# Where a transform's stores, its statistics and a copy of the solved block stand in a spectral convolution kernel

## The reference

```python
m = mean(g, axis=(2, 3, 4)); s = var(g, axis=(2, 3, 4))      # g: 32 groups of channels
v = (g - m) / sqrt(s + eps)
xfft = rfft2(pad(v, 1), norm='ortho')                        # 34 x 18 frequencies
vfft = rfft2(weight, s=(34, 34), norm='ortho')               # 128 x 127 at each frequency
wfft = vH @ vfft
wfft = wfft + mean(diagonal(wfft)) * 1e-5 * I
ortho = I - 2.0 * (vfft @ solve(wfft, vH))                   # cut to 128 x 128
z = irfft2(ortho @ xfft, norm='ortho')[:, :, 1:-1, 1:-1] + bias
return x + z
```

## Time and profile before

| | us |
|---|---|
| median of 3 runs | 3135.11 |
| lowest, highest | 3126.38, 3148.89 |
| the profiled execution | 3139.82 |
| its span, first to last instruction | 3137.1 |
| PE busy | 2606.8 (83%) |
| VectorE busy | 2014.0 (64%) |
| ScalarE busy | 1269.0 (40%) |
| GpSimd busy | 742.2 (24%) |

### The profile page before, as it was taken

One profiled execution on the slowest core, in us unless ns is written; L12 is line 12 of the kernel. 1 busy time (PEld: TensorE's weight loads), 2 busy tenths in 40 slices (PEclk: granted clock), 3 DMA queues, 4 the chain that ended last, 5 costly groups with the idle time before them and its releaser, 6 DMA issues. The chain is left out here.

```text
span 3137.1 us, 89161 instructions
## 1 busy us (share of the span) xinstructions
PE 2606.8 (83%) x38281; PEld 2133.8 (68%) x38281; DVE 2014.0 (64%) x3842; ACT 1269.0 (40%) x2963; POOL 742.2 (24%) x1307
## 2 busy tenths in 40 slices
PE   3994919889999888998886968778888879959999
PEld 3663915555666677877775747566676768859999
DVE  5453710779788787787778889697887782003333
ACT  0441402443534255555533534343454444632221
POOL 0340000312121042332431414031343242520000
PEclk7897969989999899999988989797988899976787
DMA  4348073314231064754733516060231232566662
GB/s 171 104 110 149 2 121 67 123 56 163 68 113 40 15 129 81 139 110 80 158 67 62 109 29 135 3 136 13 93 95 53 65 120 77 164 140 162 169 168 92
DMA packets 562599, 310.00 MB, mean 99 GB/s; under 512 B 484616, under 2 KB 495496, under 8 KB 561368
## 3 DMA queue, kind: packets, MB, share of 16 engines
q1 hardware_dynamic: 520896, 183.58, 28.5%
q0 software_dynamic: 41312, 120.73, 11.4%
HBM read 162.85 MB, written 141.30 MB: 97 GB/s over the span
## 5 line engine op out<-in xcount | busy, mean ns | idle before, releaser
L1386 DVE SCALAR_TENSOR_TENSOR arena<-arena,psum 128x512 f32<-128x512 f32 (+2 forms) x608 | 399.0, 719 | 280.2 <-PE psum L1016 279.9
L1349 DVE TENSOR_TENSOR arena<-arena 128x960 f32<-128x960 f32 (+24 forms) x480 | 420.2, 876 | 16.6
L1344 DVE TENSOR_TENSOR arena<-arena 128x960 f32<-128x960 f32 (+8 forms) x600 | 403.9, 723 | 8.3
L953 PE MATMUL psum<-arena 128*32 128x256 f32 (+1 forms) x2904 | 263.9, 430 | 90.9 <-DMA arena<-plain 73.9
L995 PEld LDWEIGHTS psum<-arena 32*32 32x32 f32 x9280 | 160.5, 118 | 256.9 <-issue 240.4
L871 POOL COPY arena<-arena 128x512 f32<-128x512 f32 (+2 forms) x160 | 87.1, 594 | 1040.0 <-ACT arena L1159 1040.0
L1016 PE MATMUL psum<-arena 32*128 32x64 f32 x9280 | 313.1, 282 | 9.8 <-ACT arena L1180 9.8
L1016 PEld LDWEIGHTS psum<-arena 32*128 32x128 f32 x9280 | 291.7, 197 | 34.5 <-ACT arena L1180 20.4
L995 PE MATMUL psum<-arena 32*32 32x64 f32 x9280 | 187.0, 235 | 135.9 <-DVEq L1378 125.7
L957 PE MATMUL psum<-arena 128*32 128x256 f32 (+1 forms) x3696 | 264.5, 373 | 0.0
L1159 ACT COPY arena<-arena 32x128 f32<-32x128 f32 (+3 forms) x496 | 222.2, 448 | 31.4 <-DVE arena L1386 12.5
(11 more groups left out here) (121 smaller groups left out, 4764.9 us busy)
## 6 DMA issues: line engine op xcount, KB each, us to landing
blocks<-arena POOLq DMA_DIRECT2D x145, 256.0 KB, 2.5
arena<-blocks SPq DMA_DIRECT2D x290, 128.0 KB, 2.8
kept<-arena POOLq DMA_DIRECT2D x145, 256.0 KB, 3.0
arena<-kept SPq DMA_DIRECT2D x145, 256.0 KB, 2.8
xhat<-arena SPq DMA_DIRECT2D x32, 580.0 KB, 13.0
arena<-xhat SPq DMA_DIRECT2D x580, 32.0 KB, 2.6
yhat<-arena POOLq DMA_DIRECT2D x290, 64.0 KB, 2.3
arena<-x SPq DMA_DIRECT2D x8, 2048.0 KB, 11.7
```

Of the source, the lines that this page charges most:

```text
L953: pe.matmul(columns[quadrant(p)].rearrange("p (a k) n -> p a k n", k=m), K["ident"][:, quadrant(p)], spread(base[:, 0:m, :], 1, n), start= ...
L1344: ins = dve.tensor_tensor(pr, spread(R[:, t, :, :, j], 3, 2 * w_), both, ALU.mult)
L1349: link(dve.tensor_tensor(rest, rest, pr[:, :, h], op))
L1386: ins = dve.scalar_tensor_tensor(old, old, K["mask"][:, piv:piv + 1], upd_bank(u, c)[:, 0:L * n].rearrange("p (t n) -> p t n", n=L), ALU.m ...
```

## The change

In block 1 VectorE makes the statistics first and the shift matrices after them. `eps_all` moves from block 1 to block 2, behind `norm(1)` of the first half. SP does not wait at the end of block 2 any more, and does not store the second half there; it stores it in the solver, behind the second load of tables, and the loads for `pre`, ScalarE's `copy_blocks` and VectorE's first `place` wait for all stores. `HOME` turns around, so that group a lies at the high end of `M`, and `ce` moves to the low end, so that forming does not touch `xs`. `copy_p` and `copy_q` move from GpSimd to ScalarE.

```diff
-HOME = [0, 82]
+HOME = [NQ - 82, 0]
...
+        def store_half(sp, h):
+            for p in range(NP):
+                for r in range(2):
+                    lo = 2 * B * (p % LB) + B * r
+                    sp.dma_start(xhat[p // LB, h, lo:lo + B, :], xs[p * B:p * B + B, r, :, :].rearrange(
+                        "i f b -> i (f b)")).then_inc(s_stored, 16)
...
                     ident_d = spread(K["ident"], 1, ND)
+                    statistics(dve, 0, link, 0)
                     dve.wait_ge(s_const, 32)
                     dve.wait_ge(s_a_copied, nbank)
...
                     dve.tensor_tensor(shift_sb, shift_sb, diag, ALU.add).then_inc(s_shift, 1)
-                    statistics(dve, 0, link, 0)
-                    dve.wait_ge(s_tab, 16)
-                    link(dve.tensor_tensor(eps_prod, eps_tab, spread(e_d, 1, NQ), ALU.mult))
-                    dve.tensor_reduce(eps_all, eps_prod, AX.X, ALU.add)
...
-                    for h in range(2):
-
-                        sp.wait_ge(s_s2_cp, 3 * (h + 1) * HALF)
-                        for p in range(NP):
-                            for r in range(2):
-                                lo = 2 * B * (p % LB) + B * r
-                                sp.dma_start(xhat[p // LB, h, lo:lo + B, :], xs[p * B:p * B + B, r, :, :].rearrange(
-                                    "i f b -> i (f b)")).then_inc(s_stored, 16)
-                    sp.wait_ge(s_stored, 16 * NP * 2 * 2)
+                    sp.wait_ge(s_s2_cp, 3 * HALF)
+                    store_half(sp, 0)
...
+                            if c == 0:
+                                dve.wait_ge(s_eps, 16)
+                                link(dve.tensor_tensor(eps_prod, eps_tab, spread(e_d, 1, NQ), ALU.mult))
+                                link(dve.tensor_reduce(eps_all, eps_prod, AX.X, ALU.add))
...
         a = Carve(BASE_SOLVE)
+        NCE = NT
+        ce = a(NCE, SP_, 2 * B)
+        M_AT = a.at
         M = a(RESIDENT, QUAD, L)
...
                         if kind in ("form", "pre"):
+                            if kind == "pre" and k == 0:
+                                sp.wait_ge(s_stored, 16 * NP * 2 * 2)
                             for n, (of, _, first, _, _, _) in enumerate(loads):
                                 if of == kind and lo <= first < hi:
                                     load_tables(n)
+                                if n == 1 and at == 0:
+                                    store_half(sp, 1)
...
                         elif kind == "mid":
-                            pool.wait_ge(S["upd_copied"], 2 * before("sweep", at))
...
                             for m in range(lo, hi):
-                                copy_p(m)
-                                if m > lo:
-                                    store_part(m - 1)
-                            store_part(hi - 1)
+                                store_part(m)
                         elif kind == "final":
-                            pool.wait_ge(S["s_done"], before("mid", at))
-                            pool.wait_ge(S["upd_copied"], 2 * before("sweep", at))
-                            for m in range(lo, min(lo + 4, hi)):
-                                copy_q(m)
                             for m in range(lo, hi):
                                 store_y(m)
-                                if m + 4 < hi:
-                                    copy_q(m + 4)
...
+                    def copy_p(m):
+                        if m >= 2:
+                            act.wait_ge(S["s_done"], m - 1)
+                        src = M[:, home(mid_quads[m]), :, :]
+                        dst = emb[:, m % 2, 1].rearrange("p f q r m -> p (f q) r m")[:, :, 0, :]
+                        act.copy(dst, src.rearrange("p f n -> p (f n)").rearrange("p (a b) -> p a b", b=B))
+                        act.copy(work[:, m % 2, :, 0:L], src).then_inc(S["p_copied"], 1)
+
+                    def copy_q(m):
+                        src = M[:, home(final_quads[m]), :, :].rearrange("p f n -> p (f n)").rearrange("p (a b) -> p a b", b=B)
+                        dst = q_emb[:, m % 4].rearrange("p f q r m -> p (f q) r m")[:, :, 0, :]
+                        act.copy(dst, src).then_inc(S["q_copied"], 1)
...
                         elif kind == "pre":
+                            act.wait_ge(s_stored, 16 * NP * 2 * 2)
...
                             copy_b(lo)
+                            copy_p(lo)
                             copy_j(lo)
                             for m in range(lo, hi):
                                 copy_t(m)
                                 if m + 1 < hi:
                                     copy_j(m + 1)
+                                    copy_p(m + 1)
                                 copy_s(m)
...
                                 for m in pairs[n + 1] if n + 1 < len(pairs) else ():
                                     copy_jq(m)
+                                    copy_q(m)
...
-                        if sj >= NCE:
+                        if sj < NCE:
+                            dve.wait_ge(s_stored, 16 * NP * 2 * 2)
+                        else:
                             dve.wait_ge(S["u_done"], set_jobs[sj - NCE][3])
```

More of the change, by code:

```diff
@@ L261, in build @@
         s_x = [ctx.enter_context(nc.semaphore(f"s_x{i}")) for i in range(4)]
-        s_mv = ctx.enter_context(nc.semaphore("s_mv"))
+        s_mv, s_eps, s_stored = (ctx.enter_context(nc.semaphore(n)) for n in ("s_mv", "s_eps", "s_stored"))
+        def store_half(sp, h):
[4 more added lines that the diff above has]
+                        "i f b -> i (f b)")).then_inc(s_stored, 16)
         def load_x(sp, h, q):
@@ L680, in build @@
         assert early.at <= a.at
-        early = Carve(BASE_SOLVE + HOME[1] * QUAD * L)
+        early = Carve(M_AT + HOME[1] * QUAD * L)
         tiles += [table(early) for _ in range(4)]
@@ L1279, in _ @@
                             act.wait_ge(S["formed"], before("form", at))
-                            act.wait_ge(S["upd_done"], before("sweep", at))
+                            act.wait_ge(S["upd_copied"], 2 * before("sweep", at))
                             copy_b(lo)
+                            copy_p(lo)
                             copy_j(lo)
```

28 lines of the change are left out of this document (7 added, 21 removed).

## The result

The changed kernel takes **3025.52 us** (median of four runs, 3022.56 to 3029.43); the kernel before, in runs on the same chip, took 3142.0 (3126.38 to 3153.34). The ratio is 0.9633, with a 95% interval of 0.9585 to 0.9681. The forecast was 3012 (from a median before of 3135.1), the range 2988 to 3050. The profiled execution took 3026.17 around a span of 3023.4 us, 113.7 us less than the span before.

The account below looks back on a forecast made before the run. Stages run one behind another, each bound by its last-ending wait (store, statistics, VectorE's factorization, PE or ScalarE). Terms -17.8 - 64.6 + 4 - 28.8 - 9 - 7 = -123 us, from 3135.1 to 3012 us; range 2988 to 3050.

Parts of the forecast that it names:

- The first block, -17.8: Block 1: with the statistics first, as x lands, the block ends at 57.8 and not 75.6, -17.8 us.
- The epsilon work behind `norm(1)`: Transform: the 7.8 us of epsilon product and sum, moved there, cost nothing because VectorE's idleness covers them.
- The store, -64.6 and +4: Ahead of the solver: storing beside forming removes 64.6 us; PE's wait for the third table load adds 4, within 0 to 5.
- the +5: Forming: by the skill's ring-order rule the third table load is wholly behind the stores, costing +5 us, not +4.
- VectorE beside `mid`, -28.8: `mid` of group b: without GpSimd's copies, VectorE's three-set factorizations take 91.0 us as beside `pre`, -28.8 us over four.
- PE's waits to fall to 65 us: Sign in the profile after: PE's waits beside `mid` of group b, 93.4 us before, near 65 us in sum.
- ScalarE pays nothing: `mid`: the two copies, 0.70 us together, fit in ScalarE's 1.25 us idle between `copy_j` and `copy_s`, costing nothing.
- slower by ScalarE: Rival: ScalarE bounds `mid` of a and `final`; 0.9 us a copy eats the 123 us, 0.96 gives 3155; chance 0.02.
- `mid` of a, -9: Group a's four `mid` jobs: earlier `solve_b` and quicker later rounds without GpSimd's copies, together -9 us.
- The first half of the step: Start of group a's `mid` jobs: `solve_b` comes 1.7 us sooner, four times, -6.8 us.
- The second half of the step: Later rounds of group a's `mid` jobs: GpSimd, slowed by VectorE, is no longer late, some 2 us.

Follow-up runs that it names:

- experiment 3: The changed kernel with the statistics and epsilon table back at the end of block 1: 3051.04 us, ratio 0.9706 to the kernel before.
- Experiment 2: Also `copies_back`: the changed kernel with `copy_p` and `copy_q` back on GpSimd; 3074.55 us, ratio 0.9779 to the kernel before.
- 5 and 6: The changed kernel with four unused GpSimd instructions a quad added in `mid`: copies in the first, 3046.3 us; fills in the second, 3029.8 us.
- Experiment 7: The changed kernel with two or four more unread ScalarE copies to PSUM in every quad of `mid`: 3042.39 and 3086.97 us.
- warm_all: The changed kernel with constant multiplications on PE ahead of sweeps, at their ends and at the start of `mid`: 2988.22 us, ratio 0.9513.
- late_wait: The changed kernel with SP's wait for the store of the shift matrices moved from block 1 to block 2: 3022.09 us, ratio 0.9612.
- warm_most: `warm_all` and `late_wait` together, plus PE multiplications in block 1 and early block 2, but fewer behind `pre` and `form`: 3005.53 us, ratio 0.953.
- store_back: The changed kernel with the stores of the second half put back into the transform's block: 3079.66 us, ratio 0.9793 to the kernel before.

## Why the prediction was right

*The first block, -17.8.* Right to 0.1 us, and its steps to 0.3 (34.88, 49.83, 57.67). The epsilon work behind `norm(1)` is hidden as argued (experiment 3).

*The store, -64.6 and +4.* The hole shrank by 64.7 us. The wait for the third load was 2.35 us and not 4, within the 0 to 5: PE wanted it 61.8 us after its start (I had 62.3), and had it at 64.1, where I had put the landing between 56.7 and 66.7. That is less than the +5 that I had worked out by the Trainium skill, page "DMA: Bandwidth & Descriptors", section "Queues, rings and completion order". The stores do stand in the load's way: its first two issues take SP 6.33 us, against 1.69 in the earlier trace rows. Whether its packets passed any of theirs, no row shows.

*VectorE beside `mid`, -28.8.* Right: -27.1 in the jobs' lengths, 28.9 when the copies go back. Experiment 2 shows that the copies are the cause; 5 and 6 show that GpSimd's reading accounts for about half of it, and the other half is open. I expected PE's waits to fall to 65 us; they fell to 73.1, since PE itself gets through its quads 7 us sooner without its waits for GpSimd.

*ScalarE pays nothing.* Right in after: a round of `mid` stays at 3.60 us with 0.64 idle. Experiment 7 measures the reserve as one more copy: half of the idle time that the view shows is not to be had. My rival "slower by ScalarE" needed 0.9 us a copy; a copy takes 0.31.

*`mid` of a, -9: the step that failed.* It came to -2.0. The first half of the step holds: `solve_b` starts 2.90 us into the job, 4.64 before, the 1.7 that I had. Over the four jobs it starts 6.4 us sooner, where I had 6.8. But the first `copy_s` comes at 9.4 instead of 10.2 in this job, and 2.6 us sooner in all four together. PE waits 2.57 us ahead of the job for VectorE's update, the clock has fallen by then, and comes back 8.4 us after the start of the job, as it did before (8.2). What the change brings forward, the eight L1045, now falls in that time and takes 2.20 us, where L1062 took 1.27. Windows of that job, after and then before, up to where the clock rises and behind it:

```profile
1155.96:1164.40 8.44, 7.62 (x24) 6.36 (x25) 6.59 (x9) 4.49 (x12) 2.26 (x4) 0.50 0.15 23
1164.40:1165.40 1.00, 1.00 (x9) 1.00 (x8) 0.90 (x5) 0.08 (x1) 0.00 (x0) 1.00 0.00 0
```
```profile
1226.20:1234.30 8.10, 5.53 (x16) 4.39 (x17) 6.28 (x8) 2.79 (x7) 5.49 (x8) 0.50 0.01 2
1234.30:1236.30 2.00, 2.00 (x15) 1.91 (x15) 1.84 (x6) 0.60 (x1) 0.00 (x0) 0.97 0.60 91
```

In all twelve such jobs of before, after and `copies_back` the clock comes back 8.2 to 12.9 us into the job, and the first `copy_s` 0.4 to 2.0 us behind that. In `warm_all`, where it is up at the start, the first `copy_s` comes at 7.2 us in this job, and the stage is 10.5 us shorter than before. No kernel with the copies on GpSimd was run with the clock kept up, so that the 9 us would have come then is argued and not shown. The second half of the step, 2 us in later rounds, did not come: behind the first `copy_s` the rounds of the four jobs take 299.0 us, and 298.3 before. The rounds over 3.6 us are still there, and ScalarE's waits ahead of `copy_t` for the store to `kept` are 16 (13.6 us), 10 before (9.1 us). I had costed the steps of a job at fixed lengths and had not looked at the level at which each runs.

*What the sum left out.* The transform took 2.7 us longer, the inverse 2.4, the sweeps of three sets 12.2, those of two sets 15.8 less. None of these has to do with a changed line. That they cancel to 1.5 us is luck. The sweeps follow the time at 1.2 GHz: in after 132.7 us of the 428.5 and 34.8 of the 306.3, in before 108.7 of 416.3 and 71.2 of 322.1. The transform does so too: the clock is back 29 us behind its start before and 38 in after. Which sweeps are hit differs between kernels that share this code (`late_wait`: 413.4 and 332.8 us). Why a given sweep is hit and another not stays open. That runs of one kernel differ by 7 to 40 us would fit it, but only one run of each has a trace.

*The number.* The sum was -123 us and the span fell by 113.7: 7 of the missing us are `mid` of a, the rest small shares of the others. The forecast of 3012 lies 13.5 us below the median of 3025.5. Of these 6.9 come from the median before (3135.1 in three runs, 3142.0 in four) and the rest from the sum: the medians differ by 116.5 us and not by 123.

## What to carry to other kernels

Look for a barrier that waits for stores whose data the next stage does not want at once, and move the stores behind the next stage's first loads; the price is the wait of whatever is queued behind them, here 2.35 us for 64.7. When VectorE takes longer for the same instructions in one stage than in another, see what GpSimd reads there, and give its copies to ScalarE as far as its round does not grow; its idle time in a round is more than what can be used, here 0.64 us of which 0.3 were. Where PE waits for a few microseconds ahead of many small multiplications, price what follows at both clocks, and try to keep it at work in the wait.

## What the runs showed of the hardware that I had not expected

A wait of PE can cost more than its length: 4.44 us idle ahead of a sweep, and then 56.2 us for what takes 48.6 with the clock up. The price is not the same each time: before, the same sweep took 50.3 us after 3.03 us idle, 6.8 of them at 1.2 GHz. Waits that are "free" since PE is not the bound there are paid in the next stage; filling them gave 38 us, more than the copies' move in `mid` of b did. Idleness ahead is not the only cause: in the first sweep of `warm_most`, with none, the clock fell 11 us into the sweep for 13.7 us.

The clock does not come back as soon as PE is busy. At the start of the transform PE is busy for 20.0 of 20.0 us from 80 to 100, and the granted clock of that window is 0.58 in `late_wait`; it rose at 96 to 97 us in `late_wait` and after, and at 82 to 87 in eight others whose first two blocks are after's, `store_back`'s last store apart.

Four GpSimd fills a quad cost VectorE next to nothing (90.9 to 91.5 us where 91.0 to 91.1 are the rule), four copies of the same size 3.6 to 4.0 us in 91, the two real copies of the same bytes 6.8 to 7.8.
